# Last pass of a two-layer graph kernel: the first quad of tiles handled as four single tiles

## The reference, cut to what matters

```
x = x + _L1_gnn_ref(_layernorm(x), adj, ...)
x = x + _L1_ffn_ref(_layernorm(x), ...)
# _L1_ffn_ref:
idx = jnp.argmax(xf @ router_w.T + router_b, axis=-1)
h   = relu(einsum('nd,ndh->nh', xf, W1[idx]) + b1[idx])
out = relu(einsum('nh,nhd->nd', h, W2[idx]) + b2[idx])
```

## Time and profile before

| what | value |
|---|---|
| runs | 1133.31 us median of 3 (1130.54 to 1134.15) |
| profiled execution: its own time | 1130.97 us |
| span of its trace | 1129.1 us |
| POOL busy over the span | 775.0 us (69%), its output scatters 157.4 us in 160 |
| PE busy over the span | 912.3 us (81%) |
| chain that ended last: POOL output scatters, line 530 | 13% of the span |
| last pass in the trace | first load issued at 904.66 us, first output scatter at 916.66 us, last one at 1121.90 us |

### The profile page before, as it was taken

One profiled execution on the slowest core, in us unless ns is written; L12 is line 12 of the kernel. 1 busy time (PEld: TensorE's weight loads), 2 busy tenths in 40 slices (PEclk: granted clock), 3 DMA queues, 4 the chain that ended last, 5 costly groups with the idle time before them and its releaser, 6 DMA issues. The chain is left out here.

```text
span 1129.1 us, 27365 instructions
## 1 busy us (share of the span) xinstructions
PE 912.3 (81%) x6789; PEld 816.1 (72%) x6789; DVE 788.4 (70%) x3492; ACT 706.8 (63%) x2414; POOL 775.0 (69%) x989
## 2 busy tenths in 40 slices
PE   5989889888539999999999389999997168799920
PEld 4778778777439999999999378888886056577710
DVE  6688888988739999999999248888889323322200
ACT  3998888988226556556666299999995046543300
POOL 4247776777736788877888404777788737777775
PEclk9998898989559999999999699999998589955555
DMA  9134432121187777887876202223321544333310
GB/s 213 45 97 135 129 119 72 58 63 35 47 190 201 207 211 208 208 213 202 210 206 180 67 20 58 78 80 79 87 63 40 128 122 130 99 100 102 88 44 6
DMA packets 147913, 130.88 MB, mean 116 GB/s; under 512 B 26450, under 2 KB 119484, under 8 KB 147760
## 3 DMA queue, kind: packets, MB, share of 16 engines
q1 hardware_dynamic: 125456, 93.02, 33.2%
q0 software_dynamic: 18272, 34.21, 9.0%
q10 hardware_dynamic: 4032, 1.89, 0.9%
HBM read 83.28 MB, written 49.61 MB: 118 GB/s over the span
## 5 line engine op out<-in xcount | busy, mean ns | idle before, releaser
L477 POOL DMA_INDIRECT xs<-staged,dst x256 | 256.9, 1004 | 77.1 <-issue 68.4
L1069 ACT ACTIVATE hT<-bank,wt 128x128 f32<-128x128 f32 x620 | 176.8, 368 | 131.3 <-PE bank L1276 115.8
L530 POOL DMA_INDIRECT out<-oq,xq x160 | 157.4, 984 | 63.3 <-issue 47.9
L508 POOL DMA_INDIRECT x2d<-ob,xi x155 | 161.6, 1043 | 41.4 <-issue 27.0
L1262 PE MATMUL bank<-xnT,wt 128*128 128x128 f32 x1240 | 165.9, 277 | 0.0
L1276 PE MATMUL bank<-w2s,hT 128*128 x1240 | 164.0, 275 | 0.6 <-DVE ob L953 0.5
L1262 PEld LDWEIGHTS bank<-xnT,wt 128*128 128x128 f32 x1240 | 152.7, 194 | 0.1
L1276 PEld LDWEIGHTS bank<-w2s,hT 128*128 128x128 f32 x1240 | 150.9, 192 | 1.0 <-issue 1.0
L1018 ACT ACTIVATE p<-bank,nm 128x128 f32<-128x128 f32 x256 | 102.5, 400 | 18.8 <-DVE nm L701 18.8
L980 DVE SCALAR_TENSOR_TENSOR oq<-bank,xq 128x512 f32<-128x512 f32 x40 | 27.6, 691 | 121.7 <-DMA out<-oq,xq 77.7
L1019 ACT ACTIVATE p<-bank,nm 128x128 f32<-128x128 f32 x256 | 104.1, 407 | 0.0
(11 more groups left out here) (202 smaller groups left out, 2240.2 us busy)
## 6 DMA issues: line engine op xcount, KB each, us to landing
wt<-wpd SPq DMA_DIRECT2D x155, 258.0 KB
xq<-xs SPq DMA_DIRECT2D x160, 66.0 KB
xi<-xs SPq DMA_DIRECT2D x155, 66.0 KB
xb<-x2d SPq DMA_DIRECT2D x32, 258.0 KB, 4.4
xb<-in_x SPq DMA_DIRECT2D x32, 256.0 KB, 4.2
wpd<-w1c SPq DMA_DIRECT2D x56, 129.0 KB, 3.2
xs<-staged,dst POOLq DMA_INDIRECT x256, 2.5
out<-oq,xq POOLq DMA_INDIRECT x160, 2.3
```

The lines of the kernel that those rows point to most:

```text
L477: pool.indirect_dma_start(out=xs[l], out_offset=bass.IndirectOffsetOnAxis(ap=dst[b % ND][:, c:c + 1], axis=0), in_=stag[s][:, q, 0:ROW], i ...
L508: pool.indirect_dma_start(out=x2d, out_offset=bass.IndirectOffsetOnAxis(ap=xi[t % NXI][:, ID:ID + 1].bitcast(U32), axis=0), in_=ob[:, t % ...
L530: pool.indirect_dma_start(out=orow, out_offset=bass.IndirectOffsetOnAxis(ap=xq[j % NXQ][:, q, ID:ID + 1].bitcast(U32), axis=0), in_=oq[j % ...
L1069: last = act.activation(hT[t % 2][:, j, :], HID[t % 2][:, j, :], ACT.Gelu, bias=wt[t % NW][:, c:c + 1])
```

## The change

Quad 0 is taken out of the loops and handled as four single tiles, with steps of 128 columns. Each of its loads counts a semaphore of its own (`first_in0` to `first_in3`). DVE scales the four tiles one by one, then does their four outs. On PE the tiles go through T, H and Y one step apart; the stages use two PSUM banks each by turns (`TQ2`: banks 0 and 5 for T; `HQ` and `YQ` as they were, but by tile). ACT copies and applies relu tile by tile, and does the copies of `vq` for quad 1 after that, not before. The semaphores `xnq`, `xq_ps`, `xnqT`, `hq_ps`, `hqT`, `yq` and `oq` count four for quad 0 and one for each later quad; `upto` gives the new index. POOL's wait on `oq` now stands ahead of every scatter, not only of the first of a quad. The loops over quads start at 1.

```diff
         TQ, HQ, YQ = bank[0], bank[1:3], bank[3:5]
+        TQ2 = (bank[0], bank[5])
...
+        def upto(j, q=3):
+
+            return q if j == 0 else j + 3
+
+        def past(eng, name, j):
+
+            if j >= 0:
+                after(eng, name, upto(j))
...
-                sp.dma_start(xq[j % NXQ][:, q, :], xs1[bass.ds(row[t % 8], P), :]).then_inc(sem(f"tile_in{j % NXQ}"), 16)
+                landed = f"tile_in{j % NXQ}" if j > 0 else f"first_in{q}"
+                sp.dma_start(xq[j % NXQ][:, q, :], xs1[bass.ds(row[t % 8], P), :]).then_inc(sem(landed), 16)
...
             for j in range(QUADS):
-                after(pool, "oq", j)
                 for q in range(4):
+                    after(pool, "oq", upto(j, q))
                     pool.indirect_dma_start(out=orow, out_offset=bass.IndirectOffsetOnAxis(
                         ap=xq[j % NXQ][:, q, ID:ID + 1].bitcast(U32), axis=0),
                         in_=oq[j % NOQ][:, q, :], in_offset=None, bounds_check=NTOK - 1,
...
-            for i in range(QUADS + 2):
+            for q in range(4):
+                dve.wait_ge(sem(f"first_in{q}"), 16)
+                dve.tensor_scalar(xnq[:, q, :], xq[0][:, q, 0:P], xq[0][:, q, RS:RS + 1], None, ALU.mult).then_inc(sem("xnq"), 1)
+            for q in range(4):
+                after(dve, "yq", upto(0, q))
+                dve.scalar_tensor_tensor(oq[0][:, q, :], YQ[q % 2][:, q * P:(q + 1) * P], 0.0, xq[0][:, q, 0:P], ALU.max,
+                                         ALU.add).then_inc(sem("oq"), 1)
+            for i in range(1, QUADS + 2):
                 j = i
...
-                    dve.wait_ge(sem(f"tile_in{j % NXQ}"), 16 * (len(range(j % NXQ, NTILE[0], NXI)) + 4 * (j // NXQ + 1)))
-                    after(dve, "xq_ps", j - 1)
+                    dve.wait_ge(sem(f"tile_in{j % NXQ}"), 16 * (len(range(j % NXQ, NTILE[0], NXI)) + 4 * (j // NXQ + (j % NXQ > 0))))
+                    past(dve, "xq_ps", j - 1)
                     dve.tensor_tensor(xnq[:, :, :], xq[j % NXQ][:, :, 0:P],
                                       xq[j % NXQ][:, :, RS:RS + 1].broadcast_to([P, G, P]), ALU.mult).then_inc(sem("xnq"), 1)
                 j = SECOND.get(i, -1)
-                if j >= 0:
-                    after(dve, "yq", j)
+                if j > 0:
+                    past(dve, "yq", j)
...
-                after(act, "hq_ps", j - NVQ)
-                after(act, "hqT", j - NVQ)
+                past(act, "hq_ps", j - NVQ)
+                past(act, "hqT", j - NVQ)
...
-                after(act, "hq_ps", j)
-                after(act, "yq", j - 2)
+                past(act, "hq_ps", j)
+                past(act, "yq", j - 2)
...
             expert = []
             copies(0)
+            for i in range(5):
+                if i < 4:
+                    after(act, "xq_ps", upto(0, i))
+                    act.activation(xnqT[:, i * P:(i + 1) * P], TQ2[i % 2][:, i * P:(i + 1) * P], ACT.Copy).then_inc(sem("xnqT"), 1)
+                if i > 0:
+                    q, c = i - 1, slice((i - 1) * P, i * P)
+                    after(act, "hq_ps", upto(0, q))
+                    act.activation(hqT[0][0:H1, c], HQ[q % 2][0:H1, c], ACT.Relu, bias=vq[0][0:H1, q, H1:H1 + 1]).then_inc(sem("hqT"), 1)
             copies(1)
-            for i in range(QUADS + 1):
-                if 2 <= i + 1 < QUADS:
+            for i in range(1, QUADS + 1):
+                if i + 1 < QUADS:
                     copies(i + 1)
                 if i < QUADS:
-                    after(act, "xq_ps", i)
-                    after(act, "hq_ps", i - 1)
+                    past(act, "xq_ps", i)
+                    past(act, "hq_ps", i - 1)
                     act.activation(xnqT[:, :], TQ[:, :], ACT.Copy).then_inc(sem("xnqT"), 1)
-                if i == 0:
-                    inner(0)
-                elif i > 1:
+                if i > 1:
                     inner(i - 1)
...
-            for i in range(QUADS + 2):
+            expert = column(mybir.EngineType.PE, 1, 1, 0, (E1 - 1) * VW)
+            for i in range(6):
+                if i < 4:
+                    after(pe, "xnq", upto(0, i))
+                    if i > 1:
+                        after(pe, "xnqT", upto(0, i - 2))
+                    pe.transpose(TQ2[i % 2][:, i * P:(i + 1) * P], xnq[:, i, :], ident[:, :]).then_inc(sem("xq_ps"), 1)
+                if 0 <= i - 1 < 4:
+                    q, c = i - 1, slice((i - 1) * P, i * P)
+                    if q == 0:
+                        after(pe, "vq", 0)
+                    after(pe, "xnqT", upto(0, q))
+                    if q > 1:
+                        after(pe, "hqT", upto(0, q - 2))
+                    pe.matmul(HQ[q % 2][0:H1, c], vq[0][:, q, 0:H1], xnqT[:, c], start=True, stop=True, skip_group_check=True).then_inc(sem("hq_ps"), 1)
+                if 0 <= i - 2 < 4:
+                    q, c = i - 2, slice((i - 2) * P, (i - 1) * P)
+                    after(pe, "hqT", upto(0, q))
+                    if q > 1:
+                        after(pe, "oq", upto(0, q - 2))
+                    pe.matmul(YQ[q % 2][:, c], hqT[0][0:H1 + 1, c], vflat[0:H1 + 1, bass.ds(expert[q] + (H1 + 1), P)], start=True,
+                              stop=True, skip_group_check=True).then_inc(sem("yq"), 1)
+            for i in range(1, QUADS + 2):
                 j = i
                 if j < QUADS:
-                    after(pe, "xnq", j)
-                    after(pe, "xnqT", j - 1)
+                    past(pe, "xnq", j)
+                    past(pe, "xnqT", j - 1)
                     turn(TQ, xnq, "xq_ps")
                 j = SECOND.get(i, -1)
-                if j >= 0:
+                if j > 0:
...
-                    after(pe, "hqT", j)
-                    after(pe, "oq", j - 2)
+                    past(pe, "hqT", j)
+                    past(pe, "oq", j - 2)
...
-                    after(pe, "xnqT", j)
-                    after(pe, "hqT", j - 2)
+                    past(pe, "xnqT", j)
+                    past(pe, "hqT", j - 2)
```

## The result

| | before | changed |
|---|---|---|
| median of the runs | 1133.26 us (5 runs, 1130.32 to 1134.15) | 1138.70 us (5 runs, 1138.37 to 1139.69) |
| ratio to before | | 1.0051, 95% interval 1.0027 to 1.0076 |
| profiled execution, its span | 1130.97 us, 1129.1 us | 1139.5 us, 1137.6 us |

The changed kernel is slower by 0.5%, outside the range that was forecast. Measured again later beside the kernel before, it was 1.0038 (1.0023 to 1.0054).

A forecast was written before the change was run, and what follows sets the result against it. POOL's scatters bound the kernel: quad 1's start plus 155 steps. Quad 1's first scatter at 921.6 us against 922.13 gains 0.5 us: 1133.31 - 0.5 = 1132.8 us, own range 1131.4 to 1134.2, full range 1129.6 to 1136.0 us.

The forecast's parts named there:

- POOL sets the pace from the fifth scatter on, and quad 1 has no slack: On POOL: 155 steps of 1.289 us after quad 1's start set the end; POOL already waits about 0.3 us.
- The gap: POOL's wait before its first scatter moves behind the fourth, an idle time of about 6 us.
- From X at the high clock: Quad 1 on DVE, PE and ACT: from X to the start of T2 3.14 us, at PE's high clock.
- second rival: PE's low clock stays until Y1: quad 1 at POOL at 925.8 us, 3.7 us lost, median 1137.0; chance 0.08.
- The argument against it: On PE: the trace of before had gaps of 0.78 and 0.24 us in this stretch, and the clock rose.
- X: End of quad 0's fourth out on DVE, before which scale 1 cannot start: 912.9 us, floor 911.5, ceiling 914.0.
- a tile's own path: Tile 0 through DVE, PE and ACT, load to out: 3.49 us; POOL starts at 910.7 us, 5.9 us earlier.
- met waits are free: POOL's 117 already met waits cost nothing, at most 0.01 us each, 1.2 us in all.

The follow-up runs named there:

- the early runs: Changed kernel with scale 1 between second and third out of quad 0, T1 ahead of last two Y: 0.9978, 0.9998, 0.9998 (slower machine), 1.0027 (faster).
- The fill run: Changed kernel with idle products in PE's gaps, ahead of T1 and behind T1 and T2: ratios 0.9994 (slower machine), 1.0010 (faster).
- the runs of 70 products: Changed kernel with 70 idle PE products ahead of the last pass, ratio 1.0007; the same with scale 1 and T1 let in earlier, 0.9996.
- the run with the gap: Changed kernel with 45 and 12 idle PE products ahead of the last pass, a gap between them: ratio 1.0016.

## Why the prediction was wrong, step by step

- **Right: POOL sets the pace from the fifth scatter on, and quad 1 has no slack.** The fifth scatter moved by +4.8 us, and the pass grew by 6.0. The gap went where the prediction said, behind the fourth scatter; it was 9.9 us and not 6.
- **The step that failed: "From X at the high clock".** The forecast took the clock of before for quad 1, since T1 comes at about the time of the rise. It stayed low through T1, H1, T2, H2, T3 and Y1. From scale 1 to the fifth scatter it took 929.46 - 916.71 = 12.75 us; the prediction had 8.7, and 8.7 + 4.2 = 12.9 for its second rival. In its place the runs show the low clock through all of quad 1, worth 4.0 us. The mechanism and its price were those of the rival, and the chance of 0.08 was far too small. The argument against it, that before had gaps too and the clock rose all the same, compared gaps of 0.78 and 0.24 us in work by quads with work by tiles and a gap of 0.98 us behind it.
- **Also mis-sized: X.** The forecast had scale 1 at 8.2 us after the first load; it was 9.5. PE's single steps queue wider than I took from the rows. T to H is 0.40 us, H to the next step 0.57, and Y to the next step 0.72, where I had 0.42 for each pair:

```profile
911.52 0.64 PE L1321 MATMUL bank<-xnqT,vq 128*32 128x128 f32 x2
912.09 0.80 PE L1327 MATMUL bank<-vt,hqT 33*128 x2
912.81 0.47 PE L1313 MATMUL bank<-ident,xnq 128*128 128x128 f32 x1
913.21 0.64 PE L1321 MATMUL bank<-xnqT,vq 128*32 128x128 f32 x2
```

  A pair's two weight loads take 0.50 us for Y (128 columns each) and 0.18 us for H (32 columns each) in this trace, and no [rows] had a Y at the low clock alone; that this is the cause of the longer step was not tested. Together the term is 9.5 - 8.2 = 1.3 us. The order's queue ahead of scale 1 is then worth 1.6 us, shown by the early runs.
- **Right: a tile's own path.** Tile 0's scatter came at 6.8 us after the first load against 6.0 forecast; copy 0.28, relu 0.36, scale 0.29, out 0.29 against 0.30, 0.34, 0.30, 0.30; only Y was 0.80 and not 0.63.
- **Right: met waits are free,** by POOL's gaps. One remainder: the 155 steps take 200.9 to 201.3 us in five traces of changed orders on the faster machine, and 199.8 to 200.6 in three of before's. POOL's scatters are busy a little longer in the first (158.9 us in 160, 157.4 in the trace of before), its gaps are not. The means of the two groups differ by 0.8 us. What makes it I have not settled.
- **The sum as it came out:** -0.5 forecast, +1.3 for X, +4.0 for the clock: +4.8 us.
- **The rule of the Trainium skill,** "TensorE: Matmul & The Clock Gate", section "A second HAM failure mode: psum-queue depth-cycling", pointed the right way: it has small idle times between groups of work that cycle through PSUM banks, and a clock that swings between its levels. The fill run agrees that the idle times matter (clock up at 12.8 us in place of 33). They are not the whole of it, since from 929 to 940 us PE had no idle time and the clock stayed low; and no run here tells whether the two banks matter.

What stays open: which of the gaps counts. Filling those behind quad 0 was enough to bring the clock up early, but in two traces with the clock high at T0 (the runs of 70 products in the changed orders) it fell while the single tiles were still at work. And the one late rise of before's order shows that the early rise is likely there, not certain.

No version beat the kernel before on the faster machine. The nearest is the changed kernel with its gaps filled, at 1.0010 (0.9999 to 1.0021), which can't be told from no change.

## What to carry to other kernels

Before a pipeline's first piece is made smaller, ask what the second piece waits for: here the output engine got its first tile 5 us sooner and had no use for it, since the second quad was no sooner. Splitting PE's work at the start of a stage also thins it out just where the clock is low, and here a clock that came up 24 us later cost 4.0 us, where the split was forecast to give 0.5. A time taken from rows at the high clock holds only if the change leaves PE's work as dense as it was.

## What the runs showed of the hardware that was not expected

- Windows in which the profile has PE busy all the time don't always bring the clock up soon: 929 to 940 us of the changed kernel (11 of 11 us) stand at 0.50. It is not the changed order alone: in the order of before, with only the waits added, 944 to 951 us (7 of 7 us) stand at 0.50 too.
- Idle work that ended 5 us ahead of the next work was worth nothing: in the run with the gap the clock of the changed kernel was at 1.00 until about 925 us and at 0.50 when the first tile landed.
- The same program took 1133 us on one chip and 1195 to 1201 us on three others, and there the whole loss was hidden (ratio 1.0003). POOL waited for outs throughout the pass there, which fits, but no run tests it as the reason.
